# Turning tiles in the scores' banks, one place earlier in the step, in an attention block with recurrent feed-forward

## What is computed

```python
xn = layernorm(x)
# attention: 16 query heads of 64, 4 key/value heads, window of 512 and 4 sink columns
q, k, v = xn @ Wq.T, xn @ Wk.T, xn @ Wv.T
att = softmax(where(mask, q @ k.T / 8, -inf));  s = (att @ v) @ Wo.T
# feed-forward: one row per batch, four recurrent steps
thought = layernorm(xn)[:, -1] @ agg_w + agg_b
for _ in range(4): thought += gelu(layernorm(thought) @ d1_w + d1_b) @ d2_w + d2_b
out = xn + sigmoid(xn @ gate_w + gate_b) * (thought @ bc_w + bc_b)
y = x + s * silu(layernorm(out))
```

## Time and profile before

| what | value |
|---|---|
| median of 3 runs | 2227.8 us (2224.46 to 2233.3) |
| the profiled execution, its own time | 2227.23 us |
| its span, first to last instruction | 2225.5 us |
| PE busy, of the span | 2156.4 us, 97% |
| DVE busy | 1462.0 us, 66% |
| ACT busy | 840.2 us, 38% |
| mean granted clock of PE | 0.991 |

### The profile page before, as it was taken

How to read it: one execution, slowest core, us unless ns; L and a number is a source line. 1 busy time by engine, 2 the same in 40 slices (tenths; PEclk the granted TensorE clock), 3 DMA queues, 4 the chain that set the end, 5 groups by cost and what they waited for, 6 DMA issues and landing times. The chain is left out here.

```text
span 2225.5 us, 35922 instructions
## 1 busy us (share of the span) xinstructions
PE 2156.4 (97%) x13433; PEld 1607.4 (72%) x13433; DVE 1462.0 (66%) x3257; ACT 840.2 (38%) x1793; POOL 254.4 (11%) x518
## 2 busy tenths in 40 slices
PE   7999999999999999999999999989999999999997
PEld 6677666766766777666676666657888888888886
DVE  7466676565666756567656566665766676766767
ACT  2355554444554435455444455462111111111111
POOL 2100111010001120011101000140101100010100
PEclk9999999999999999999999999999999999999999
DMA  7496469434458634546853455645333324243331
GB/s 256 155 284 217 133 203 289 166 113 135 153 166 277 201 129 139 168 140 200 280 179 110 129 180 180 217 137 196 129 135 119 141 104 151 96 149 109 136 138 52
DMA packets 174383, 366.57 MB, mean 165 GB/s; under 512 B 13320, under 2 KB 111880, under 8 KB 159904
## 3 DMA queue, kind: packets, MB, share of 16 engines
q1 hardware_dynamic: 168240, 348.30, 46.7%
q0 software_dynamic: 5568, 14.79, 2.0%
q10 hardware_dynamic: 432, 1.57, 0.2%
HBM read 284.79 MB, written 79.72 MB: 164 GB/s over the span
## 5 line engine op out<-in xcount | busy, mean ns | idle before, releaser
L812 ACT ACTIVATE pt<-t_ps 128x512 f32<-128x512 f32 x432 | 238.2, 595 | 468.9 <-PE t_ps L1096 468.3
L1029 PE MATMUL j_ps<-x_hi,w 128*128 128x512 f32 x1232 | 414.0, 406 | 0.0
L821 ACT ACTIVATE probs<-probs,neg_max 128x660 f32<-128x660 f32 (+5 forms) x512 | 356.7, 703 | 57.1 <-DVE neg_max L1350 57.0
L1350 DVE CUSTOM_DVE_ANT_0 probs<-s_ps,mask 128x660 f32<-128x660 f32 (+5 forms) x512 | 322.3, 667 | 72.0 <-PE s_ps L1064 69.7
L1748 PE MATMUL out_ps<-wo,w 128*128 128x512 f32 x1536 | 353.5, 389 | 2.6 <-DVE w L1805 2.6
L1748 PEld LDWEIGHTS out_ps<-wo,w 128*128 128x128 f32 x1536 | 288.2, 188 | 62.8 <-issue 3.0
L1748 PE MATMUL gate_ps<-x_hi,w 128*128 128x512 f32 x1024 | 281.6, 391 | 4.8 <-PEq L468 4.8
L1029 PEld LDWEIGHTS j_ps<-x_hi,w 128*128 128x128 f32 x1232 | 231.9, 191 | 51.3 <-issue 3.8
L1096 PE MATMUL t_ps<-ident,probs 128*128 128x128 f32 x1728 | 244.8, 283 | 17.3 <-DVE x_lo L1338 11.8
L1064 PEld LDWEIGHTS s_ps<-k_hi,q 64*128 64x128 f32 x1664 | 159.8, 185 | 136.6 <-issue 80.1
L1064 PE MATMUL s_ps<-k_hi,q 64*128 64x330 f32 (+5 forms) x1664 | 251.6, 330 | 3.9 <-DVE q L1322 1.4
(11 more groups left out here) (182 smaller groups left out, 2317.2 us busy)
## 6 DMA issues: line engine op xcount, KB each, us to landing
fw<-in_L_ffn_d_w_dram SPq DMA_DIRECT2D x128, 1024.0 KB, 5.2
w<-WT SPq DMA_DIRECT2D x36, 1024.0 KB, 4.9
w<-XS SPq DMA_DIRECT2D x64, 512.0 KB, 6.4
XS<-x_hi SPq DMA_DIRECT2D x32, 512.0 KB, 4.7
XS<-x_lo SPq DMA_DIRECT2D x32, 512.0 KB, 6.2
Y<-y SPq DMA_DIRECT2D x256, 64.0 KB, 2.6
b_x<-in_L_attn_x_dram SPq DMA_DIRECT2D x32, 512.0 KB, 4.2
b_y<-Y SPq DMA_DIRECT2D x32, 512.0 KB, 6.4
```

The costliest lines, as they stand in the source:

```text
L812: act.activation(pt[:, m % PT_SLOTS, :, :], bank[:, :].rearrange("p (h q) -> p h q", q=P), ACT.Copy).then_inc(pt_ready, 1)
L821: act.activation(probs[:, slot, 0:width], probs[:, slot, 0:width], ACT.Exp, bias=neg_max[:, slot:slot + 1], scale=-1.0, accum_out=row_sum[ ...
L1029: last = pe.matmul(bank_of((kind, b, n)), w[:, slot, wp * C + c * P:wp * C + c * P + P], xs[:, c, bass.ts(ch, BANK)], start=i == 0, stop=i ...
L1350: dve.tensor_tensor_reduce(out=probs[:, slot, 0:width].rearrange("p (a n) -> p a n", a=parts), in0=s_ps[head % 2][:, :].rearrange("p (a n) ...
```

## The change

The turned halves go to the first bank of `s_ps[0]` and of `s_ps[1]` instead of the `t_ps` banks, and `turn_later` stands ahead of place 2 instead of behind it. Its two halves now wait for the masks of heads 2 and 3 of the same step, and the first scores of the next step wait for both low halves, where the first two turns of probabilities no longer do. On ACT `turned_high` comes ahead of `take_place(2)`; on DVE `turned_low` comes ahead of `normalise`, of the thought's part and of `take_place(2)`.

```diff
-        def x_bank(u, half):
+        def x_bank(half):
-            return t_ps[(turns_before(u) + half) % 2][:, :]
+            return s_ps[half][:, 0:BANK]
...
 # scalar, step
                     exponentials(b, s, 3)
-                    take_place(2)
                     if turned_in(b, s):
                         for half in range(2):
                             turned_high(u, turned_in(b, s), half)
+                    take_place(2)
                     take_place(3)
...
 # tensor, turn_later
                     for half in range(2):
-                        wait_taken(*turn_two_ago(u, half))
+                        pe.wait_ge(masked, GROUP * u + 3 + half)
                         if n:
                             pe.wait_ge(x_taken, 2 * n - 2 + half + 1)
...
 # tensor, scores
                     if u or pair:
                         pe.wait_ge(masked, GROUP * u + 2 * pair)
+                    item = turned_in(*divmod(u - 1, UNITS)) if u else None
+                    if item and pair == 0:
+                        pe.wait_ge(x_taken, 2 * turned_no(item) + 2)
...
 # tensor, turn_probs
-                    item = turned_in(*divmod(u, UNITS))
-                    if item and i < 2:
-                        pe.wait_ge(x_taken, 2 * turned_no(item) + i + 1)
...
 # tensor, step
                     turn_two(4)
-                    fill(2)
                     if turned_in(b, s):
                         turn_later(u, turned_in(b, s))
+                    fill(2)
                     if u:
                         values(u - 1)
...
 # vector, step
                     divide_pair(b, s, 1)
+                    if turned_in(b, s):
+                        for half in range(2):
+                            turned_low(u, turned_in(b, s), half)
                     if ahead is not None:
                         normalise(b + 1, ahead)
                     if b and s == 0:
                         apply_thought(b)
                     take_place(2)
-                    if turned_in(b, s):
-                        for half in range(2):
-                            turned_low(u, turned_in(b, s), half)
                     take_place(3)
```

More of the change, by code:

```diff
@@ L795, in turned_high @@
                         act.wait_ge(w_stored[weight_slot(t)], 16 * stores_before(t))
-                        dst, src = w[:, weight_slot(t), bass.ts(half, BANK)], x_bank(u, half)
+                        dst, src = w[:, weight_slot(t), bass.ts(half, BANK)], x_bank(half)
                     else:
@@ L801, in turned_high @@
                         dst = x_hi[:, 4 * half:4 * half + 4, bass.ts(t, P)]
-                        src = x_bank(u, half).rearrange("p (k n) -> p k n", n=P)
+                        src = x_bank(half).rearrange("p (k n) -> p k n", n=P)
                     act.activation(dst, src, ACT.Copy).then_inc(x_high, 1)
@@ L983, in turn_later @@
                         for c in range(4):
-                            last = pe.transpose(x_bank(u, half)[:, bass.ts(c, P)], src[:, bass.ts(4 * half + c, P)],
+                            last = pe.transpose(x_bank(half)[:, bass.ts(c, P)], src[:, bass.ts(4 * half + c, P)],
                                                 ident[:, :])
@@ L1330, in turned_low @@
                         dst = w[:, weight_slot(t), C + BANK * half:C + BANK * half + BANK]
-                        src, hi = x_bank(u, half), w[:, weight_slot(t), bass.ts(half, BANK)]
+                        src, hi = x_bank(half), w[:, weight_slot(t), bass.ts(half, BANK)]
                     else:
@@ L1336, in turned_low @@
                         at = (slice(None), slice(4 * half, 4 * half + 4), bass.ts(t, P))
-                        dst, src, hi = x_lo[at], x_bank(u, half).rearrange("p (k n) -> p k n", n=P), x_hi[at]
+                        dst, src, hi = x_lo[at], x_bank(half).rearrange("p (k n) -> p k n", n=P), x_hi[at]
                     dve.tensor_tensor(dst, src, hi.bitcast(F32), ALU.subtract).then_inc(x_taken, 1)
```

## The result

The changed kernel takes 2218.78 us (median of 11 runs, 2215.52 to 2225.78); the kernel before, timed beside it, takes 2228.65 us (11 runs, 2223.37 to 2233.3). The ratio is 0.996, with a 95% interval of 0.9949 to 0.9972: some 9 us less, which is small but clear of the scatter, and near the 2217.5 forecast. The profiled execution's span is 2217.1 us, 8.4 under the 2225.5 of before.

What follows compares the result with a forecast made beforehand. PE, busy 97%, was held by waits for low halves, mostly at step 26's start, and half clock behind them. Gains of 9.25 us there plus 0.6 elsewhere, 9.85 off 2227.2, gave 2217.5; range 2212 to 2227.

Steps and rivals of the forecast that it cites:

- (1): Step 24: turns ahead of place 2 let the tile's load go out 1.7 us earlier and land at 346.5.
- first rival: Load must outlast the `w<-WT` megabyte, so lands only 0.5 us earlier; gain 3.4 us, 2224; chance 0.25.
- The 0.9 left over in batch 2: Statistics' wait for the tile's load in batch 2, forecast to shrink from 2.60 us by 1.7.
- (2): Before step 26, batch 0: low halves come directly behind the divisions, so x_lo ends at 350.9.
- (3): Step 26: wait moves ahead of the scores, 1.35, 1.35 and 2.25 us; gains 3.25, 3.15 and 2.85, sum 9.25 us.
- (5): Turns wait for their own step's masks: net -0.15 in step 26, -0.55 in step 27, -0.4 in step 28.
- the half clock priced into batch 2: Step 26 of batch 2: a 2.25 us wait was taken to bring the half clock once, costing 1.5 us.
- third rival: Half clock stays in all three batches after waits as forecast; gain 6.8 us, 2220.5; chance 0.15.
- (4): Turns no longer wait for a `t_ps` bank: gains of 0.75 in step 29, 0.3 in step 23, 0.25 in step 22.
- (6): Seven weight steps, tightest step 10: nothing gained or lost, up to 0.1 us lost.
- The sum: All gains over three batches: 9.25 us at step 26 plus 0.6 from the other steps, 9.85 us.
- five rivals: Load hardly earlier 0.25, wait only moved 0.1, half clock in all batches 0.15, more than forecast 0.2, slower 0.05.

Runs made afterwards that it cites:

- e4: Changed kernel with the two loads of the values' weights issued a step later each (steps 25 and 26); 2233.33 us against 2226.06, ratio 1.0031.
- e7: Changed kernel with SP's stores of the turned tile issued ahead of the values' weights in steps 24 and 25; 2215.81 us against 2226.99, ratio 0.9947.
- e10: The same kernel as e8, run again beside e9 on one chip; 2212.49 us against 2230.12, ratio 0.9924.
- e1: Kernel before with one edit: DVE's low halves directly behind the second divisions; 2219.18 us against 2226.06, ratio 0.9966.
- e3: Changed kernel's banks and semaphores, with the orders of before on PE, ACT and DVE; 2247.48 us against 2226.06, ratio 1.0088.
- e2: Changed kernel's orders on PE, ACT and DVE, but the tile turned in the banks of before, with their waits; 2229.86 us against 2226.06, ratio 1.0013.
- e5: Changed kernel with the turns of probabilities ahead of the scores at steps 24 and 26 of batches 0 to 2; 2219.84 us against 2226.99, ratio 0.9962.
- e6: Changed kernel with turns of probabilities first in steps 24 and 26 to 29, place 2 ahead of the tile's turns in 26 to 28; 2212.3 us, ratio 0.993.
- e8: The edits of e6 and e7 together on the changed kernel; 2210.76 us against 2226.99, ratio 0.992.
- e9: Kernel before with two edits: e1's low halves behind the divisions and e7's stores ahead of the weights' megabyte; 2222.04 us against 2230.12, ratio 0.997.

## Why the prediction held, point by point

**What bounds the kernel** was read rightly: the six waits for the low half and the half clock behind three of them were the money, 17.7 us in all; 12.0 us came.

**(1) The load.** Its landing was forecast for 346.5, which is 14.3 into step 24 as that step stood before; it came at 14.56, 14.90 and 14.95. That is near, but for another reason than the step gave, and so in part luck. The step took 1.7 us off the issue and left the duration at 7.3. The duration isn't the load's own: it is 3.9 to 5.4 us where the megabyte goes out later (e4 and e7 to e10, with one of 6.4 in e7), 7.5 to 7.9 after, 6.0 to 6.2 in e1, where the load goes out 3.3 to 3.4 us behind the megabyte instead of 2.3, and 4.5 to 5.4 in e3, where it is 5.5 behind.

What moved the landing was that SP's queue got to `w<-WT` 1.5 to 2.1 us earlier, in good part since its stores wait for `x_taken`. The prediction looked at POOL's queue and not at what SP's stores wait for. e1 shows it most clearly: there the load is issued no earlier at all, the megabyte 0.8 to 1.5 earlier, and the load lands 1.4 to 2.1 us earlier. So the first rival had the mechanism right, and only its premise, that the megabyte stays where it was, failed: in the seven kernels that have both under way (before, after, e1, e2, e3, e5, e6), the load landed 0.4 to 2.5 us behind the megabyte in all 21 cases. The Trainium skill ("DMA: Bandwidth & Descriptors", Queues, rings and completion order), which the prediction weighed against that rival, lets the load have its turns beside the other queue. The traces agree in so far as the load isn't held up entirely: it took 4.0 to 5.1 us in e4 and 7.5 to 7.9 beside the megabyte. But taking turns doesn't mean that 1.7 earlier out is 1.7 earlier in, and that was the prediction's own step. The 0.9 left over in batch 2 was 0.61, and batches 0 and 1 had 0.23 and 0.56 where none was forecast.

**(2) and (3) The low halves, and the wait ahead of the scores.** 1.56, 1.90 and 1.93 us for a forecast of 1.35, 1.35 and 2.25. Steps 25 and 26 together are shorter by 2.19, 1.71 and 3.73 us; with the 0.7 of (5) taken out the gains of (3) are 2.9, 2.4 and 4.4 for 3.25, 3.15 and 2.85, in all 9.8 for 9.25. The terms of the batches were off and offset each other, which is luck: the half clock priced into batch 2 didn't come after 1.93 us. The third rival is answered: waits of 1.56 to 1.93 us with eight turns soon behind them left the clock at 1.00 in all three batches. The Trainium skill ("TensorE: Matmul & The Clock Gate", Part 4) has it that a turn doesn't count as activity of PE like a matmul does, and the half clock that the prediction took from this for all three batches didn't come. The prediction found no row on that rule, but the trace of the kernel before has some, at its start:

```profile
12.32 1.91 PE L947 MATMUL s_ps<-ident,xn 128*128 128x128 f32 x8
...
21.65 1.06 PE L947 MATMUL s_ps<-ident,pt 128*128 128x128 f32 x8 [0.33 <-DVE pt L106]
```

Up to 16.2 PE had done nothing but turns, each of them 0.21 us behind the one before where they follow each other; there the first record of the granted clock begins, at 1.00, and later eight turns take 1.06 us instead of 1.91. So here the clock went from half to full behind turns alone.

**(4) The banks' waits that go.** Step 29: 0.88 to 0.94 for 0.75. Step 23: 0.32 for 0.3. Step 22: 0.21 for 0.25.

**(5) The masks.** 0.72 in step 26, as forecast. In step 27 the old wait of 0.65 at the start shrank to the 0.1 that was forecast, and the turns lost 0.4 for 0.55 (the 0.27 in the rows above, and the rest at their second half: the eight take 1.23 us instead of 1.10), so that the step itself is 0.28, 0.21 and 0.13 shorter. Step 28 lost 0.33 for 0.4. Step 24, which had no term, gained 0.1. Steps 22 to 24 and 27 to 29 and the 0.7 of step 26 together gave 0.7 a batch instead of 0.2.

**(6) The weight steps.** Steps 2 to 21 of batch 0 take 207.79 us, before 207.72: nothing.

**The sum** was 9.85; the stretches gave 12.0 and the rest of this profile gave 3.6 back, so that 2217.5 against 2218.8 is closer than the working deserved. (The chances of the forecast and the five rivals add up to 1.05 and not to 1, so that each is a little too high.) What the prediction didn't ask is which edit earns the sum. DVE's order alone is enough for it (e1: 13.7 us in the stretches). The new place of the turns needs the new banks (e2 against the kernel after: 11.5 us), and the two together bring nothing beyond e1, until place 2 and the turns of probabilities are set right around them (e6, e8).

What stays open: why a half-clock stretch stands at a batch's start in one profile and not in another; why e1 gains less by the times than in the stretches; and how much of the 9.6 us between e9 and e10 is `fw` and how much the banks; no kernel had e8's orders in the old banks.

## What to carry to other kernels

When a wait ends in one engine's list, look first at the order in that list: two instructions moved past some 1.4 us of other work gave all that a change of buffers, waits and three engines' orders gave. When a transfer seems slow, look at what else is under way when it lands, and at what each queue's earlier entries wait for; moving one megabyte aside only helps until it meets the next. And price a refill of a wait by the next thing that the waiting engine needs of the same supplier: PE could do something else during 1.9 us, and gained 0.36, since DVE was the chain.

## What was not expected of the hardware

A wait of PE between 2.0 and 2.6 us can be followed by half clock or not: it was after 2.02 and 2.58 us in e3, in each batch, and after 2.17 there in batches 0 and 1 but not in 2; in e2 a wait of 2.24 us was followed by full clock in batches 0 and 1 and by half clock in batch 2; and after the 2.60 us in e9 the clock stayed full. After 1.93 us and less at these places it never fell, and after 2.94 us and more it always did.

The load of half a megabyte took 3.9 to 5.4 us (6.4 once) with the megabyte `w<-WT` behind it or a step away, and 7.5 to 7.9 in the kernel after, with that megabyte issued 2.3 us ahead of it on another queue. The megabyte took 9.1 to 9.5 us then and 8.1 to 9.6 in e7, where the load was ahead of it; and `fw`, issued 4.6 us behind the megabyte in e9, took 10.5.
